# Down projection on one core: a store and a load of residual rows moved behind the last load of hidden blocks

## The reference

```python
xq = _act_fake_quant(x, clip_x[0])
gate = jnp.einsum('bsh,ih->bsi', xq, _weight_fake_quant(w_gate))
up = jnp.einsum('bsh,ih->bsi', xq, _weight_fake_quant(w_up))
h = _act_fake_quant(jax.nn.silu(gate) * up, clip_down[0])
return jnp.einsum('bsi,hi->bsh', h, _weight_fake_quant(w_down))
...
x = x + _L0_xattn_ref(...)
x = x + _L0_ffn_ref(_layernorm(x, axis=-1), ...)
```

## Time and profile before

| | |
|---|---|
| median of 3 runs | 1272.61 us (1272.20 to 1272.67) |
| the profiled execution | 1272.64 us, of which 1270.8 us are the span of its trace |
| mean granted clock of TensorE | 1.00 of full speed |
| PE busy | 1249.2 us (98%) |
| DVE / ACT / POOL busy | 1104.5 / 796.9 / 288.7 us |
| moved by DMA | 241.74 MB, 190 GB/s over the span |

### The profile page before, as it was taken

One profiled execution on the slowest core, in us unless ns is written; L12 is line 12 of the kernel. 1 busy time (PEld: TensorE's weight loads), 2 busy tenths in 40 slices (PEclk: granted clock), 3 DMA queues, 4 the chain that ended last, 5 costly groups with the idle time before them and its releaser, 6 DMA issues.

```text
span 1270.8 us, 20478 instructions
## 1 busy us (share of the span) xinstructions
PE 1249.2 (98%) x7576; PEld 586.4 (46%) x7620; DVE 1104.5 (87%) x2127; ACT 796.9 (63%) x1209; POOL 288.7 (23%) x227
## 2 busy tenths in 40 slices
PE   6999999999999999999999999999999999999998
PEld 4644444444444444444444445444444444444443
DVE  7776888988988898898889859899999999799998
ACT  7578686567658756756775672333433333399994
POOL 2104331342144134214403420000000000013223
PEclk9999999999999999999999999999999999999999
DMA  8275257246255353363562391386656652489997
GB/s 306 75 242 182 34 158 220 79 133 202 66 173 166 105 191 105 116 216 84 154 220 92 100 267 69 99 278 265 235 204 265 225 189 83 149 291 424 422 423 301
DMA packets 171108, 241.74 MB, mean 190 GB/s; under 512 B 122096, under 2 KB 141312, under 8 KB 154880
## 3 DMA queue, kind: packets, MB, share of 16 engines
q1 hardware_dynamic: 171008, 240.43, 56.2%
HBM read 120.86 MB, written 90.57 MB: 166 GB/s over the span
## 4 chain that ended last, share of the span: by engine, by line
PE 73%; ACT 9%; DVE 8%; DMA 6%; issue 2%; SPq 2%; POOL 1%; DVEq 0%; ACTq 0%; POOLq 0%
PE bank L1690 10%; PE bank L1694 10%; PE po L77 9%; PE po L79 8%; PE po L78 8%; PE ring L79 7%; PE ring L78 7%; PE ring L77 7%; ACT hb L1527 5%; DMA xa<-x_rows_d 2%; DMA out_dram<-xa 2%; PE ring L1086 2%; PE bank L1731 1%; PE ring L1113 1%; DMA x<-in_x_dram 1%
## 5 line engine op out<-in xcount | busy, mean ns | idle before, releaser
L1511 ACT ACTIVATE sg<-bank,gate_scale 128x512 f32<-128x512 f32 x176 | 120.8, 687 | 184.0 <-PE bank L1690 174.0
L77 PE MATMUL ring<-yT,M 128*128 128x512 f16 x512 | 194.1, 379 | 0.0
L78 PE MATMUL ring<-yT,M 128*128 128x512 f16 x512 | 194.0, 379 | 0.0
L79 PE MATMUL ring<-yT,M 128*128 128x512 f16 x512 | 194.0, 379 | 0.0
L77 PE MATMUL po<-VW,p 128*128 128x512 f16 x480 | 182.2, 380 | 0.0
L78 PE MATMUL po<-VW,p 128*128 128x512 f16 x480 | 181.9, 379 | 0.0
L79 PE MATMUL po<-VW,p 128*128 128x512 f16 x480 | 181.9, 379 | 0.0
L1690 PE MATMUL bank<-xqT,w 128*128 128x512 bf16 x682 | 176.8, 379 | 1.5 <-DMA xqT<-xq 0.7
L1694 PE MATMUL bank<-xqT,w 128*128 128x512 bf16 x682 | 176.7, 379 | 0.7
L481 ACT ACTIVATE p<-E 128x512 f16<-128x512 f32 x120 | 74.6, 624 | 132.7 <-DVE E L678 132.6
L1731 PE MATMUL bank<-w 128*128 128x512 bf16 x690 | 151.8, 379 | 3.1 <-DVE w L1646 2.3
(11 more groups left out here) (266 smaller groups left out, 1945.9 us busy)
## 6 DMA issues: line engine op xcount, KB each, us to landing
hidden<-hb SPq DMA_DIRECT2D x11, 2816.0 KB, 8.9
xa<-x_rows_d SPq DMA_DIRECT2D x28, 1024.0 KB, 6.0
hb<-hidden SPq DMA_DIRECT2D x22, 1024.0 KB, 14.8
x<-in_x_dram SPq DMA_DIRECT2D x16, 1024.0 KB, 5.3
value_fold<-E SPq DMA_DIRECT2D x64, 256.0 KB, 2.5
VW<-value_fold SPq DMA_DIRECT2D x16, 1024.0 KB, 6.1
x_rows_d<-x SPq DMA_DIRECT2D x16, 1024.0 KB, 4.2
out_dram<-xa SPq DMA_DIRECT2D x11, 1024.0 KB, 10.3
```

Source lines behind the costliest of these rows:

```text
L77: nc.tensor.matmul(out, a_hi, b_hi, start=first, stop=False)
L78: nc.tensor.matmul(out, a_hi, b_lo, start=False, stop=False)
L79: return nc.tensor.matmul(out, a_lo, b_hi, start=False, stop=last)
L1511: nc.scalar.activation(sg[:, n % 4], pg[n % 4][:], ACT.Silu, scale=gate_scale[:, n % FT:n % FT + 1]).then_inc(silus, 1)
```

## The change

Two transfers of SP's list are issued later: the store of block 8 and the load of the rows of block 11. Both now stand behind the three pieces of `load_h(15)`. The store's code becomes a function `store(q)`; what it issues is the same.

```diff
+        def store(q):
+
+            slot = r_slot(q)
+            sp.wait_ge(added, 2 * q + 2)
+            sp.wait_ge(added_too, 2 * q + 2)
+            if slot == ODD:
+                sp.dma_start(og[taken_as(q)][:, 0:2], spare_pair).then_inc(out_stored[slot], 16)
+                for t in (2, 3):
+                    sp.dma_start(og[taken_as(q)][:, t], r_tile(slot, t)).then_inc(out_stored[slot], 16)
+            else:
+                sp.dma_start(og[taken_as(q)], xa[slot]).then_inc(out_stored[slot], 16)
+
         for q in range(NG):
             if q + 6 < NG:
                 load_h(q + 6)
+            if q + 7 == NG - 1:
+                continue
+            if q + 6 == NG - 1:
+                load_r(q + 2)
+                store(q - 1)
             slot = r_slot(q)
             if q < NG - 1:
-                sp.wait_ge(added, 2 * q + 2)
-                sp.wait_ge(added_too, 2 * q + 2)
-                if slot == ODD:
...
-                else:
-                    sp.dma_start(og[taken_as(q)], xa[slot]).then_inc(out_stored[slot], 16)
+                store(q)
             else:
```

More of the change, by code:

```diff
@@ L1464, in on_sync @@
                 load_h(q + 6)
+            if q + 7 == NG - 1:
[3 more added lines that the diff above has]
+                store(q - 1)
             slot = r_slot(q)
             if q < NG - 1:
-                sp.wait_ge(added, 2 * q + 2)
-                sp.wait_ge(added_too, 2 * q + 2)
-                if slot == ODD:
-                    sp.dma_start(og[taken_as(q)][:, 0:2], spare_pair).then_inc(out_stored[slot], 16)
-                    for t in (2, 3):
-                        sp.dma_start(og[taken_as(q)][:, t], r_tile(slot, t)).then_inc(out_stored[slot], 16)
-                else:
-                    sp.dma_start(og[taken_as(q)], xa[slot]).then_inc(out_stored[slot], 16)
+                store(q)
             else:
```

## The result

The changed kernel takes 1274.51 us (median of 18 executions, 1273.05 to 1276.57), the kernel before, beside it, 1272.19 us (18 executions, 1270.96 to 1273.39). The ratio is 1.0019, with a 95% interval of 1.0013 to 1.0025: 2.3 us slower, close to the forecast (1274.8), and just inside the bound of 0.2%, which the interval reaches beyond. Timed again beside the last experiment it was 1275.33 us against 1272.07, ratio 1.0022 (1.0013 to 1.0031), which is 2.8 us; the medians are 3.3 us apart.

A forecast was written before the change was run, and what follows sets the result against it. PE, DVE, ACT and the full DMA queue run close together, with late rows 12 stopping PE once near the end. New stop 3.40 less old 1.25 gives +2.15 us on 1272.64: 1274.8 us, range 1273.0 to 1276.3.

The forecast's parts named there:

- Both terms of the sum: PE's new stop in block 13, 3.40 us, less its old stop in block 14, 1.25 us: +2.15 us.
- SP and the queue: Store 9, rows 12 and store 10 issued and landing as before; store 8 late, rows 13 at 1247.9: no cost.
- Rows 11 later by 4.34 us: Overtaken by 2816 KB and overtaking 1024 KB, rows 11 land at 1235.6 in place of 1231.25.
- the price by size: DMA queue first in, first out, always full: about 2.45 us for 1024 KB, 6.81 for block 15's `hb`.
- 5.32 us to the second piece: DVE's time from rows 11 landing to block 13's second rounded piece, its addition slow beside POOL's: ready at 1240.9.
- The new stop of 3.40 us: PE stops before matmul 4 of block 13, starting it at 1240.98 in place of 1237.58.
- The old stop of 1.25 us, saved: PE's stop before matmul 4 of block 14 disappears, by a thin 0.3 us, as rows 12 are no longer late.
- Rows 11 hardly late (first rival): Rows 11 less than 0.9 us late, so the time stays 1272.6 us; chance 0.08.
- DVE does not recover (second rival): DVE's delayed turn costs 0.5 to 1 us more, PE stops again in block 14: +2.4 to +2.9 us; chance 0.11.
- the 8.22 and 0.15 of the forecast: DVE's undisturbed turn from `scale_down` to the second piece, 8.22 us, plus up to 0.15 for POOL's later start.
- The clock (third rival, 0.05): PE falls to 1.2 GHz after the new stop: 1276.5 us, or 1284.3 if over a whole block; chance 0.05.
- the 3.44 us before the first matmul: PE's idle time at the trace's start, followed by granted clock 1.00; taken to show a stop costs only itself.

The follow-up runs named there:

- the last experiment: The full change, with POOL's additions to rows 11 held back until DVE has rounded the second piece of block 13: 1273.86 us, ratio 1.0011 to the kernel before.
- The store alone: Against the kernel before, only store 8 moved behind block 15's `hb` load, rows 11 staying ahead of it: 1271.21 us, ratio 0.9995.
- With two pieces ahead: Against the kernel before, rows 11 and store 8 behind two of the three pieces of block 15's `hb`, ahead of the third: 1272.69 us, ratio 1.0007.
- the load alone: Against the kernel before, only the load of rows 11 moved behind block 15's `hb`, store 8 staying ahead: 1278.76 us, ratio 1.0052.
- the three kernels whose profile had no stop, or next to none: Only store 8 moved (1271.21 us); full change with DVE's turn 12 and 13 additions behind the roundings (1271.84); block 15's `hb` behind store 9 and rows 12 (1271.35).
- the run with SP's order of before and late additions: The kernel before, with DVE's additions of turns 12 and 13 moved behind the roundings of the next block's second and third piece: 1271.60 us, ratio 1.0000.

## Why the prediction was right

The sum was +2.15 us and 2.32 were measured, by the mechanism that it names: rows 11 late, DVE held by them, PE stopped once in block 13. Both terms of the sum were too large for an average execution, and that they were so by nearly as much is luck. Point by point:

- **SP and the queue.** Held. Stores 8 and 9 were issued by 1216, rows 12 at 1217.86, as soon as store 7 had landed. Rows 13 were issued 8.0 us later and still landed by 1246.5, no later than the count of what is queued had said (1247.9). The store alone costs nothing measurable.
- **Rows 11 later by 4.34 us.** Nearly. Counted from the landing of store 7, rows 11 came 11.7 us after it in both profiles of before (1231.25 - 1219.54 and 1229.71 - 1217.94) and 16.4, 16.9 and 16.1 us in those of the change (the last 1235.26 - 1219.16): 4.4 to 5.2 later. With two pieces ahead 14.3 us, where the same arithmetic by size says 14.2; with the load alone 19.0, where it says 18.5. The queue keeps the order and the price by size is good to 0.8 us in the worst of these.
- **5.32 us to the second piece.** Held: 1239.61 - 1234.30 = 5.31, of which 2.1 us are shown to be the two engines side by side.
- **The new stop of 3.40 us.** Right in kind, mis-sized: 1.8, 2.9 and 3.1 us from start to start in the three profiles (the profile's 1.62, 2.71 and 2.95 and the 0.16 of the last matmul).
- **The old stop of 1.25 us, saved.** Mis-sized as well: it is not in the second profile of before, and none of the three kernels whose profile had no stop, or next to none, was measurably faster than before. Both terms came from one profile in which the queue was late. Store 7 landed there 87.3 us after the common start (1219.54 - 1132.23); in the second one 85.3 (1217.94 - 1132.64), and in the three of the change 85.3, 86.0 and 87.0. A queue later by 1 us adds 1 us to the new stop, and 1 us to the old one as long as there is an old one: it is used up when the queue is 1.25 us earlier than in the first profile, and from there on the difference shrinks. By the few profiles at hand an average execution has 2.6 us of new stop (1.8, 2.9, 3.1) and 0.5 of clock (1.54 in one of three), less 0.6 of old stop (1.25 and 0). That estimate is 2.5 us, beside the 2.3 and 2.8 of the timings. So the direction and the rough size follow from the mechanism; the hit within 0.2 us does not. The single terms were up to 1.6 us off, and the clock's loss made up for a part.
- **Rows 11 hardly late (first rival).** Not seen in any of the three profiles.
- **DVE does not recover (second rival).** Not seen: from the scaling of block 12 at 1240.46 to the second piece of block 14 at 1248.82 it took 8.36 us, the 8.22 and 0.15 of the forecast.
- **The clock (third rival, 0.05).** Underrated. I took the 3.44 us before the first matmul as proof that such a stop costs only itself. The change shows a fall after 2.95 us, in one profile of three (PEclk below 1.00 after 1241 was one of the forecast's own signs of being wrong), and the load alone one after 4.59. The idle stretch at a program's start was no guide to one between dense matmuls. The start does not even look the same from execution to execution. In the first profile of the change PE stopped for 1.95 us before 13.28, and the granted clock (before the last two numbers of the window) was 0.71 behind it; the first profile of before, with a stop of 1.11 us there, has 1.00 in that window:

```profile
13.28 2.69 PE L1231 MATMUL ring<-ident,E 128*128 128x128 f32 x16 [1.95 <-DVE E L830]
...
15.00:20.00 5.00, 4.28 (x28) 3.38 (x27) 3.08 (x9) 4.08 (x5) 0.00 (x0) 0.71 1.03 414
```

How often the clock falls behind the new stop in the timed executions is open. They have no trace, and their mean granted clock does not tell: it was 0.998 in the first profile, without a fall at the stop, and 0.999 in the third, with one. The spread of the change (3.5 us, against 2.4 of before) fits both this and the queue.

Why the queue is up to 2.2 us earlier or later from one execution to the next stays open (store 7 landed between 85.3 us and, in the run with SP's order of before and late additions, 1219.07 - 1131.56 = 87.5). SP's list of transfers is the same up to that point in all these kernels.

## What to carry to other kernels

When one queue is full for a long stretch, the landing of a load is set by the bytes issued ahead of it: count them, and put the load whose consumer has no slack ahead of those that have (here `hb` had over 6 us, rows 11 some 1 us). Ask what stands behind the waiting instruction on its in-order engine: the addition to rows 11 was needed by nobody soon, the rounding behind it was.

A stop read from one profile is one draw. Before a sum takes credit for removing it, look at how late its cause is in other executions; a change that removes a stop that is there one time in several gains what it is on average. And a stop of about 3 us on TensorE can cost half as much again through the clock.

## What the runs showed of the hardware

- The granted clock of TensorE fell to 0.50 at the end of a stop of 2.95 us and stayed at 0.50 to 0.52 for the next 3.4 us, at a price of 1.54 us; after a stop of 2.71 us in another execution it stayed at 1.00; after one of 4.59 us it was 0.51 over the next 6.0 us, at a price of 2.80 us. At the program's start, among smaller matmuls, a stop of 1.95 us was followed by a granted clock of 0.71 over 15 to 20 us.
- Under a full queue one transfer of 1024 KB more or less ahead of a load moved its landing by some 2.6 us: rows 11 landed 11.7 us after store 7, 14.3 with 1024 KB more ahead of them, and 19.0 with 2816 KB more.
- Two additions of 128 x 512 in float32 on VectorE took 2.38 us beside GpSimd's and 1.29 us alone; GpSimd's two took 3.46 us beside them and 2.50 alone.
- The same DMA list reached the same point up to 2.2 us earlier or later from execution to execution (85.3 to 87.5 us after the same matmul), though the queue moved about 420 GB/s in all of them.
